# Attention steps of an MoE + attention + FFN kernel: ScalarE's copy of the turned weights moved ahead of the two exponentials of its step

## Chip, cores and metric

The kernel runs on one core of a Trainium2 chip. The metric is the device time of one execution in microseconds (us); lower is better. Five engines work side by side, each on its own in-order list of instructions, and they wait for each other by semaphores: TensorE (PE), VectorE (DVE), ScalarE (ACT), GpSimd (POOL), and SyncE (SP), which issues transfers.

## What is computed

The reference is a transformer block over 8 sequences of 512 tokens with 256 features: a mixture of experts with a ternary projection, then the attention that this change touches, then a quantised FFN. The attention has 16 heads of 64 features that share one key and one value (and a null key and value in front), a bias for each head, a causal mask and a padding mask:

```python
q = (xn @ Wq).reshape(b, n, H, DH).transpose(0, 2, 1, 3) * scale
kv = xn @ Wkv
k, v = (kv[..., :DH], kv[..., DH:])
...
sim = jnp.einsum('bhid,bjd->bhij', q, k)
...
sim = sim + bias
...
attn = jax.nn.softmax(sim, axis=-1)
out = jnp.einsum('bhij,bjd->bhid', attn, v)
out = out.transpose(0, 2, 1, 3).reshape(b, n, INNER)
out = out @ Wo
return layernorm(out, g_out)
```

## The kernel before

The program runs in stages: experts (to about 480 us of the profiled span), attention (`attention_phase`, about 480 to 1320 us), the two halves of the FFN (the rest). Matrices are fp32.

The attention phase works through 8 batches (one sequence each) of 32 steps. Four steps (`i % 4` = 0, 1, 2, 3) make one pair of heads; a step handles one block of 128 queries for both heads (`hh` = 0 and 1). By the causal mask a block needs 128, 512, 256 or 384 keys, in that order of the four steps (`ORDER = (0, 3, 1, 2)`). Batch 0 and batch 7 are written out by themselves, the six between them run in a hardware loop of two batches a turn. Every engine has the steps written out in the same order, and the stages of one block are spread over steps:

- step i: PE computes the scores of both heads (L1180, L1181) into `psS` (`ps_y` in the profile), one half for each head. DVE adds the bias and takes the row's extreme (`biased_max`, L1031, result `att_top`). ACT takes the exponential in place with a sum (`exps`, L893). PE may compute the scores of step i + 1 for a head only when DVE has read that head's scores of step i.
- step 4k + 3 and 4k + 4: ACT's `null_exp` (L905) and DVE's `totals` (L1047 to L1051) end the softmax sums of the pair.
- step i + 5 (`NLAG`): POOL multiplies the block by the inverse sum (`normalise`, L837).
- step i + 6 (`TLAG`): PE turns the block (`turn`, L1192, transposes of 128x128) into `psT` (`ps_up`), one half for each head. Head 0's half is copied to `pr` (`keep` in the profile) by ACT (`turned_out`, L901), head 1's half by DVE (its own `turned_out`, L1059).
- step i + 7 (`PLAG`): PE multiplies the turned weights with the values (`weighted`, L1202).

So in step i PE turns block J = i - 6 and ACT copies it. `psT` has no second buffer: PE's `turn` waits, for each half, until the copy of the block before has left it:

```python
for hh, ready in ((0, sem.pa_ready), (1, sem.pb_ready)):
    pe.wait_ge(sem.p_normed, 2 * J + hh + 1)
    if not known(J, 1):
        pe.wait_ge(ready, J)
```

`pa_ready` is counted up by ACT's copy, `pb_ready` by DVE's. Within a step PE runs scores, turn, weighted, and then, by the step, output projection (`project`, L1268), the next queries (`queries`), or one of the small products for the next batch. ACT's copy waits for `t_done` (the turn of head 0's half in the same step). Around the copy ACT has the first half of the queries (`query_hi`, L916, at the start of steps 4k + 2), the output copy (`outputs_t`, L911, at the start of steps 4k + 3), and, at the end of single steps, copies for the next batch or the one before (`null_weights` L948 in step 4, `normed_hi` L921 in 8 and 12, `keys_values` L927 in 16, ...). DVE has layer-norm pieces (L624 to L644) in steps 0 to 6 and 13 to 20.

Of the kernel before, what the change touches and what calls it, by code (L numbers as in the profile page):

```python
# [43 lines left out]
def known(v, least):  # L44

    return isinstance(v, int) and v < least
# [703 lines left out]
def attention_phase(nc, dram, w, ps, sem):  # L750
# [12 lines left out]
    TLAG, PLAG, NLAG = 6, 7, 5  # L763
    ORDER = (0, 3, 1, 2)
    with ExitStack() as ctx:
# [25 lines left out]
        def scores_of(pp, hh, q):  # L791
            return sc[:, pp, hh, CAUSAL[q]:CAUSAL[q + 1]]
# [8 lines left out]
        def lagged(b, i, lag):  # L801

            behind = i < lag
            return behind, STEPS * b + i - lag, (i - lag) % STEPS

        with nc.Block() as block:
# [80 lines left out]
            def _(act):  # L887
                def exps(I, i):
                    pp, q = i // 4 % 2, ORDER[i % 4]
                    for hh in range(2):  # L890
                        act.wait_ge(sem.ttr_done, 2 * I + hh + 1)
                        s = scores_of(pp, hh, q)
                        nc.scalar.activation(s, s, ACT.Exp, scale=-1.0, bias=top[:, pp, q, hh:hh + 1],  # L893
                                             accum_out=lsum[:, pp, q, hh:hh + 1]).then_inc(sem.exp_done, 1)

                def turned_out(J, j):
                    n = P * (ORDER[j % 4] + 1)
                    act.wait_ge(sem.t_done, 2 * J + 1)
                    if not known(J, 2):
                        act.wait_ge(sem.pv_done, J - 1)  # L900
                    nc.scalar.activation(pr[:, j % 2, 0, 0:n], psT[:, 0, 0:n], ACT.Copy).then_inc(sem.pa_ready, 1)  # L901
# [11 lines left out]
                def query_hi(n, pp):  # L913
                    act.wait_ge(sem.q_done, n + 1)
                    for hh in range(2):
                        nc.scalar.activation(q_hl[0:D, pp, hh], psB[hh * D:(hh + 1) * D], ACT.Copy  # L916
                                             ).then_inc(sem.qh_ready, 1)
# [42 lines left out]
                def step(b, i, par, behind, ahead):  # L960
                    n = PAIRS * b + i // 4
                    if i % 4 == 3 and (behind or i >= 11):
                        outputs_t(n - 2, i // 4 % 2)
                    if i % 4 == 2 and (ahead or i < STEPS - 4):
                        query_hi(n + 1, (i // 4 + 1) % 2)
                    exps(STEPS * b + i, i)
                    if i % 4 == 3:
                        null_exp(n, i // 4 % 2)
                    late, J, j = lagged(b, i, TLAG)
                    if behind or not late:  # L970
                        turned_out(J, j)
                    if behind and i == PNT + 1:
                        null_weights(b - 1)
                    if behind and i == OUT:
                        projected(b - 1)
                    if ahead:
                        for c in range(HC):
                            if i == XN[c] + 1:
                                normed_hi(b + 1, 1 - par, c)
                        if i == KV + 1:  # L980
                            keys_values(b + 1, 1 - par)
                        if i == VT + 1:
                            values(b + 1, 1 - par)
                        if i == NULL + 1:
                            null_scores(b + 1)
                        if i == NT + 1:
                            null_by_token(b + 1, 1 - par)
# [17 lines left out]
                for i in range(PLAG + 1):  # L1005
                    if i % 4 == 3:
                        outputs_t(PAIRS * B + i // 4 - 2, i // 4 % 2)
                    if i < TLAG:
                        _, J, j = lagged(B, i, TLAG)
# [1084 lines left out]
```

## Time and profile before

| | |
|---|---|
| median of 3 runs | 1495.69 us (1494.85 to 1497.03) |
| profiled execution | 1493.01 us, of it span 1491.1 us from first to last instruction |
| granted TensorE clock, mean | 0.950 |
| busy share of the span: PE, weight loads, DVE, ACT, POOL | 87%, 67%, 70%, 51%, 37% |

The profile lists for each engine its busy time, and how long it sat idle before a group of instructions and which instruction of which engine ended that idle time (the releaser). A timeline row gives the start in the span, the duration, the instruction, how many alike follow each other (x4), and in brackets the idle time before it. Matmuls are pipelined: with several in flight, a row covers them together.

### The profile page before, as it was taken

To read this page: it belongs to the slowest core of one execution; us is meant where nothing else is said; L and a number is where in the kernel's file an instruction comes from. 1 tells how busy PE (TensorE), PEld (TensorE's weight loads), DVE (VectorE), ACT (ScalarE), POOL (GpSimd) and SP (SyncE) were. 2 spreads that over 40 slices of the span, in tenths; PEclk is the share of its full clock that TensorE was granted. 3 is DMA by queue.
4 is the path that set the end of the run, shared out by engine and by line. 5 is a ranking of instruction groups with operands and counts; after the bars stand their busy time and mean duration, and the time that the engine had idled before them with its cause. 6 is when DMAs were issued, how large, how long until landed. Compare 5 with 4: busy or idle time off the path is not lost. (4 is left out here: it accounts for less than half of the span.)

```text
span 1491.1 us, 30048 instructions
## 1 busy us (share of the span) xinstructions
PE 1291.4 (87%) x8710; PEld 998.4 (67%) x8710; DVE 1040.3 (70%) x2788; ACT 760.9 (51%) x1940; POOL 554.7 (37%) x834
## 2 busy tenths in 40 slices
PE   4989989998945799999998999999999999953866
PEld 2877877787832577777776777777777788741223
DVE  5566666666554777777777778767877767762986
ACT  3222322232212566666666666666667666634853
POOL 1333232333232675444443344443443444510004
PEclk9999999999976899999999999999999999976987
DMA  6232211221125100000000000010000000202215
GB/s 224 79 107 100 85 60 54 99 85 40 46 76 184 58 1 2 1 23 9 2 29 4 2 30 2 2 31 2 1 30 2 15 2 2 73 1 66 65 48 178
DMA packets 51043, 71.55 MB, mean 48 GB/s; under 512 B 4497, under 2 KB 43665, under 8 KB 48850
## 3 DMA queue, kind: packets, MB, share of 16 engines
q1 hardware_dynamic: 50338, 69.60, 14.1%
q8 instruction: 69, 1.13, 0.3%
q14 instruction: 76, 0.62, 0.1%
q10 hardware_dynamic: 560, 0.20, 0.1%
HBM read 57.07 MB, written 12.72 MB: 47 GB/s over the span
## 5 line engine op out<-in xcount | busy, mean ns | idle before, releaser
L893 ACT ACTIVATE scores<-scores,att_top 128x128 f32<-128x128 f32 (+3 forms) x512 | 282.7, 553 | 268.6 <-DVE att_top L1031 268.5
L837 POOL TENSOR_SCALAR scores<-scores,att_rinv 128x128 f32<-128x128 f32 (+3 forms) x512 | 265.8, 536 | 203.8 <-DVE att_rinv L1049 203.8
L1031 DVE CUSTOM_DVE_ANT_0 scores<-ps_y,w_bias_b,null_s 128x128 f32<-128x128 f32 x448 | 229.6, 547 | 113.6 <-PE ps_y L1181 102.2
L261 POOL TENSOR_TENSOR act_w<-act_g,wide_w 128x512 f32<-128x512 f32 x64 | 105.6, 1650 | 282.5 <-DVE act_g L379 277.0
L1192 PE MATMUL ps_up<-ident,scores 128*128 128x128 f32 x1280 | 187.3, 275 | 26.5 <-ACT keep L901 26.1
L1202 PE MATMUL ps_a<-keep,w_val 128*64 128x128 f32 x2560 | 197.2, 284 | 0.3 <-DVE keep L1059 0.3
L1180 PE MATMUL ps_y<-k_hh,q_hl 128*128 128x256 f32 (+2 forms) x512 | 186.3, 374 | 12.7 <-DVE att_top L1031 5.9
L1192 PEld LDWEIGHTS ps_up<-ident,scores 128*128 128x128 f32 x1280 | 150.3, 140 | 49.9 <-issue 33.9
L208 ACT ACTIVATE hid_hi<-hid 128x512 fp32r<-128x512 f32 x80 | 50.5, 631 | 241.9 <-DVE hid L397 241.9
L844 POOL TENSOR_SCALAR w_q_hm<-q_hl 64x512 fp32r<-64x512 f32 x128 | 76.8, 612 | 256.2 <-ACT q_hl L916 256.2
L1202 PEld LDWEIGHTS ps_a<-keep,w_val 128*64 128x64 f32 x2560 | 135.2, 136 | 42.0 <-issue 38.1
L1181 PE MATMUL ps_y<-w_k_lm,w_q_hm 128*128 128x256 f32 (+2 forms) x512 | 162.1, 326 | 0.0
L1268 PE MATMUL ps_gate<-w_wo,o_t 128*128 128x256 f32 x512 | 145.9, 404 | 0.0
L1059 DVE COPY keep<-ps_up 128x128 f32<-128x128 f32 (+3 forms) x256 | 125.1, 489 | 12.8 <-PE ps_up L1192 7.2
L1180 PEld LDWEIGHTS ps_y<-k_hh,q_hl 128*128 128x128 f32 x512 | 97.2, 190 | 38.9 <-issue 22.2
L34 PE MATMUL ps_y<-w_down_hi,hid_hi 128*128 128x256 f32 x320 | 92.6, 289 | 26.9 <-DVE y L360 20.8
L901 ACT ACTIVATE keep<-ps_up 128x128 f32<-128x128 f32 (+3 forms) x256 | 108.0, 422 | 7.3 <-PE ps_up L1192 5.6
L379 DVE TENSOR_TENSOR act_g<-ps_gate,leak 128x512 f32<-128x512 f32 x80 | 55.3, 692 | 80.5 <-ACT leak L202 80.5
L1268 PEld LDWEIGHTS ps_gate<-w_wo,o_t 128*128 128x128 f32 x512 | 85.8, 189 | 27.6 <-issue 21.3
L1181 PEld LDWEIGHTS ps_y<-w_k_lm,w_q_hm 128*128 128x128 f32 x512 | 97.6, 191 | 7.9
L1069 DVE TENSOR_TENSOR q_hl<-ps_a,q_hl 64x512 fp32r<-64x512 f32 x128 | 88.2, 689 | 12.2 <-ACT q_hl L916 8.2
L893 ACT ACTIVATION_READ_ACCUMULATOR scores<-scores,att_top 128x1 f32 x512 | 95.8, 187 | 0.0
(236 smaller groups left out, 2596.1 us busy)
## 6 DMA issues: line engine op xcount, KB each, us to landing
wide_w<-token_w_dram SPq DMA_DIRECT2D x16, 1024.0 KB, 4.7
x_raw<-in_x_t_dram SPq DMA_DIRECT2D x8, 512.0 KB, 3.8
x_nat<-in_x_nat_dram SPq DMA_DIRECT2D x8, 512.0 KB, 4.8
x_dram<-x_nat SPq DMA_DIRECT2D x8, 512.0 KB, 2.9
w_x1t<-x_dram SPq DMA_DIRECT2D x8, 512.0 KB, 4.0
c_dram<-out_raw SPq DMA_DIRECT2D x8, 512.0 KB, 3.2
c2t<-c_dram SPq DMA_DIRECT2D x8, 512.0 KB, 3.7
x_tile<-x_dram SPq DMA_DIRECT2D x8, 512.0 KB, 4.4
```

The source lines that it names most:

```text
L34: pe.matmul(out, w_hi, x_hi, start=start, stop=False, skip_group_check=loose)
L261: nc.gpsimd.tensor_tensor(act_w[:, k % 2], act_g[:, k % 2], wide_w[:, k], ALU.mult).then_inc(sem.act_w_ready, 1)
L837: nc.gpsimd.tensor_scalar(s, s, rinv[:, pp, q, hh:hh + 1], 0.0, ALU.mult, ALU.add).then_inc(sem.p_normed, 1)
L893: nc.scalar.activation(s, s, ACT.Exp, scale=-1.0, bias=top[:, pp, q, hh:hh + 1], accum_out=lsum[:, pp, q, hh:hh + 1]).then_inc(sem.exp_don ...
L901: nc.scalar.activation(pr[:, j % 2, 0, 0:n], psT[:, 0, 0:n], ACT.Copy).then_inc(sem.pa_ready, 1)
L1031: dve.tensor_tensor_reduce(scores_of(pp, hh, q), psS[:, hh, 0:n], bias_of(w, h)[:, CAUSAL[q]:CAUSAL[q] + n], 1.0, null_s[:, par, q, h:h + ...
L1059: nc.vector.tensor_copy(pr[:, j % 2, 1, 0:n], psT[:, 1, 0:n]).then_inc(sem.pb_ready, 1)
L1180: pe.matmul(psS[:, hh, 0:n], q_hl[:, pp, hh, cols], k_hh[:, par, 0:n], start=True, stop=False)
L1181: pe.matmul(psS[:, hh, 0:n], q_hm[:, pp, hh, cols], k_lm[:, par, 0:n], start=False, stop=True).then_inc(sem.qk_done, 1)
L1192: last = pe.transpose(psT[:, hh, k * P:(k + 1) * P], s[:, k * P:(k + 1) * P], w.ident[:])
L1202: last = pe.matmul(psO[hh * D:(hh + 1) * D, cols], val[:, par, k], pr[:, j % 2, hh, k * P:(k + 1) * P], start=(k == 0), stop=(k == q))
L1268: last = pe.matmul(out, o_t[:, p % 2, cols], w.wo[:, p], start=(p == 0 and i == 0), stop=False, skip_group_check=True)
```

## The change

In ACT's `step`, `turned_out` is called before `exps` and not after it. Nothing else differs; all other engines have the same instructions in the same order.

```diff
                         query_hi(n + 1, (i // 4 + 1) % 2)
+                    late, J, j = lagged(b, i, TLAG)
+                    if behind or not late:
+                        turned_out(J, j)
                     exps(STEPS * b + i, i)
                     if i % 4 == 3:
                         null_exp(n, i // 4 % 2)
-                    late, J, j = lagged(b, i, TLAG)
-                    if behind or not late:
-                        turned_out(J, j)
```

The first place is on ACT in the batches of the hardware loop, steps 4 to 7 of a batch. L893 are the exponentials, L901 the copy out of `ps_up`, L948 and L949 the null weights of the batch before, L916 `query_hi`, L911 `outputs_t`. Before:

```order
L893 ACTIVATE scores,att_sum<-scores,att_top 128x128
L898 ISA
L901 ACTIVATE keep<-ps_up 128x256
L948 ACTIVATE w_null_nt<-ps_a 16x512
L949 ACTIVATE w_null_nt<-ps_a 16x512
L891 ISA
L893 ACTIVATE scores,att_sum<-scores,att_top 128x512
L891 REGISTER_ALU
L893 ACTIVATE scores,att_sum<-scores,att_top 128x512
L898 ISA
L901 ACTIVATE keep<-ps_up 128x384
L914 REGISTER_ALU
```

Now:

```order
L901 ACTIVATE keep<-ps_up 128x256
L891 ISA
L893 ACTIVATE scores,att_sum<-scores,att_top 128x128
L891 REGISTER_ALU
L893 ACTIVATE scores,att_sum<-scores,att_top 128x128
L948 ACTIVATE w_null_nt<-ps_a 16x512
L949 ACTIVATE w_null_nt<-ps_a 16x512
L898 ISA
L901 ACTIVATE keep<-ps_up 128x384
L891 ISA
L893 ACTIVATE scores,att_sum<-scores,att_top 128x512
L891 REGISTER_ALU
```

The copies of 256 columns (step 4) and of 384 columns (step 5) stand ahead of their step's exponentials; the null weights follow straight on the exponentials.

The second place is PE, where nothing moved: the order and the waits of two steps (4k and the start of 4k + 1) are these before and now.

```order
L1180 MATMUL ps_y<-k_hh,q_hl 128x256 [waits ttr_done]
L1181 MATMUL ps_y<-w_k_lm,w_q_hm 128x256
L1192 MATMUL ps_up<-ident,scores 128x128 [waits pa_ready,p_normed]
L1192 MATMUL ps_up<-ident,scores 128x128
L1192 MATMUL ps_up<-ident,scores 128x128 [waits pb_ready,p_normed]
L1192 MATMUL ps_up<-ident,scores 128x128
L1202 MATMUL ps_a<-keep,w_val 64x128 [waits pb_ready,pa_ready]
L1202 MATMUL ps_a<-keep,w_val 64x128 x7
L1180 MATMUL ps_y<-k_hh,q_hl 128x512 [waits ttr_done]
```

What moved is thus only when `pa_ready` is given, on which the first transpose of a turn waits.

## Rows read from the trace of the kernel before

**Rows 1.** Who waited for whom, whole run: us in total, times, longest

```profile
DVE scores L1031 <- PE ps_y L1181: 116.9, 105, 3.5
...
PE ps_up L1192 <- ACT keep L901: 26.1, 38, 1.5
```

**Rows 2.** Batch 3: length; PE, PEld, DVE, ACT, POOL busy; granted clock; DMA

```profile
793.70:897.20 103.50, 99.53 (x756) 78.99 (x757) 80.19 (x261) 67.97 (x204) 45.29 (x82) 1.00 0.04 12
```

**Rows 3.** Who waited for whom, batch 3 alone

```profile
PE ps_up L1192 <- ACT keep L901: 3.1, 4, 1.0
```

**Rows 4.** Timeline of batch 3, step 6: PE and ACT

```profile
813.39 0.39 PE L1180 MATMUL ps_y<-k_hh,q_hl 128*128 128x256 f32 x1 [0.16 <-DVE att_top L1031]
813.61 0.28 PE L1181 MATMUL ps_y<-w_k_lm,w_q_hm 128*128 128x256 f32 x1
...
814.12 0.47 ACT L901 ACTIVATE keep<-ps_up 128x384 f32<-128x384 f32 x1
...
814.74 0.52 PE L1192 MATMUL ps_up<-ident,scores 128*128 128x128 f32 x2 [0.84 <-ACT keep L901]
...
815.18 0.66 PE L1202 MATMUL ps_a<-keep,w_val 128*64 128x128 f32 x8
```

**Rows 5.** Timeline of batch 3, step 10: PE

```profile
826.73 0.28 PE L1181 MATMUL ps_y<-w_k_lm,w_q_hm 128*128 128x256 f32 x1
826.85 0.38 PE L1192 MATMUL ps_up<-ident,scores 128*128 128x128 f32 x2
827.15 0.33 PE L1202 MATMUL ps_a<-keep,w_val 128*64 128x128 f32 x2
```

**Rows 6.** Timeline of batch 3, steps 3 and 4: DVE and PE

```profile
806.14 0.69 DVE L1059 COPY keep<-ps_up 128x512 f32<-128x512 f32 x1
...
807.37 0.63 PE L1192 MATMUL ps_up<-ident,scores 128*128 128x128 f32 x4 [0.68 <-ACT keep L901]
```

**Rows 7.** Timeline of batch 3, steps 6 and 7: DVE and PE

```profile
816.91 0.29 DVE L1059 COPY keep<-ps_up 128x128 f32<-128x128 f32 x1
...
817.66 1.03 PE L1192 MATMUL ps_up<-ident,scores 128*128 128x128 f32 x8
```

**Rows 8.** Timeline of batch 3, steps 14 and 18 to 20: PE and DVE

```profile
840.05 0.52 PE L1192 MATMUL ps_up<-ident,scores 128*128 128x128 f32 x2 [0.55 <-ACT keep L901]
...
855.05 0.52 PE L1192 MATMUL ps_up<-ident,scores 128*128 128x128 f32 x2 [0.98 <-ACT keep L901]
...
860.23 0.69 DVE L1059 COPY keep<-ps_up 128x512 f32<-128x512 f32 x1
...
861.46 0.67 PE L1192 MATMUL ps_up<-ident,scores 128*128 128x128 f32 x4
```

**Rows 9.** Timeline after the last batch, where ACT waits for the turn

```profile
1311.09 1.04 PE L1192 MATMUL ps_up<-ident,scores 128*128 128x128 f32 x8
1311.73 0.60 ACT L901 ACTIVATE keep<-ps_up 128x512 f32<-128x512 f32 x1 [0.89 <-PE ps_up L1192]
```

**Rows 10.** Timeline of batch 3, steps 27 and 28: PE, ACT, DVE

```profile
883.07 1.03 PE L1192 MATMUL ps_up<-ident,scores 128*128 128x128 f32 x8
...
883.72 0.61 ACT L893 ACTIVATE scores<-scores,att_top 128x384 f32<-128x384 f32 x1 [0.72 <-DVE att_top L1031]
...
884.93 0.19 ACT L905 ACTIVATE null_p<-null_d 128x8 f32<-128x8 f32 x1
...
886.78 0.35 DVE L1031 CUSTOM_DVE_ANT_0 scores<-ps_y,w_bias_b,null_s 128x128 f32<-128x128 f32 x1
```

**Rows 11.** DVE in batch 3: its wait for the null weights, and a layer-norm piece twice

```profile
DVE w_null_nt L1063 <- ACT w_null_nt L949: 0.9, 1, 0.9
...
803.31 0.43 DVE L636 TENSOR_TENSOR w_work<-w_seed 128x4 f32<-128x4 f32 x1
...
806.92 0.16 DVE L636 TENSOR_TENSOR w_work<-w_work 128x4 f32<-128x4 f32 x1
```

**Rows 12.** Timeline of POOL around the first of those two pieces

```profile
802.68 2.07 POOL L837 TENSOR_SCALAR scores<-scores,att_rinv 128x256 f32<-128x256 f32 x4
```

## Prediction, made before the changed kernel ran

> **What bounds the kernel now.** I read the list of waits for the whole run first, then the busy times of one batch of the attention, then the timeline of that batch step by step. In the attention PE is the engine that the others follow: DVE's bias-and-extreme step waited 116.9 us in 105 places for PE's scores [rows 1], and in batch 3 PE was busy 99.53 of 103.50 us against 80.19 for DVE and 67.97 for ACT, at a granted clock of 1.00 [rows 2]. So time is gained where PE's few holes close, and only there. The largest group of holes is the one that the change aims at: before the transposes of a turn PE sat idle 26.1 us, in 38 places, until ACT's copy of the block before was out [rows 1]; in batch 3 this was 3.1 us in 4 places [rows 3].
>
> The timeline of step 6 shows how such a hole is made. PE issues its last score matmul at 813.61 and could go on to turn the next block. It starts at 814.74, because ACT's copy of step 5 only began at 814.12, behind that step's two exponentials of 512 columns, and ended at 814.59 [rows 4]. From the copy's end to the transpose is 0.15 us. An unhindered step of the same shape is step 10: last score 826.73, turn 826.85, weighted product 827.15, thus 0.42 us from score to product [rows 5]. In step 6 it is 815.18 - 813.61 = 1.57 us [rows 4]. The hole costs 1.57 - 0.42 = 1.15 us where the list says 0.84, since the pipeline has to fill again: idle time and 0.31 more. With that, all 38 holes are worth 26.1 + 38 x 0.31 = 37.9 us. This is the most that the change can return.
>
> **What the change does, part by part.**
>
> *No instruction is added or removed, and none moves on PE, DVE, POOL or SP.* ACT's copy of step i - 1 now runs before the exponentials of step i - 1. It needs only the turn of head 0's half. How soon that is shows behind the last batch, where ACT has nothing else to do: turn of 512 columns at 1311.09, copy at 1311.73, so 0.64 us later [rows 9]. The copy then ends some 1.2 us after the turn's start and is done before PE reaches the next step's turn everywhere (the steps are 2.1 us or longer: 103.50 / 32 = 3.2 on average, [rows 2]). So I take ACT's share of each hole as gone, 0 left. What takes its place is the question, because PE's turn has two halves and the second waits for DVE's copy, and PE's scores wait for DVE's extremes. Neither moves by itself. I walk through batch 3.
>
> *Steps 0 to 8.* DVE carries layer-norm pieces here and is itself close to the limit. In step 4 the hole is 0.68 us, with the turn at 807.37 [rows 6]. Transposes follow each other every 0.11 us (8 in 1.03 us less one of 0.27, over 7), so head 1's half began at 807.59. DVE's copy that it needs ran from 806.14 to 806.83 [rows 6]; with the 0.14 us of handover it could begin at 806.97. So after step 4 PE is ahead by at most 0.62 us, though the holes of steps 2 and 4 are worth more. In step 6 even that is lost: PE waits for DVE's extreme in the middle of the scores, at 813.39 [rows 4], and DVE was late by its own work. DVE gets a little earlier: its wait of 0.9 us for ACT's null weights in step 4 [rows 11] shortens by about 0.27, the distance by which the copy of 256 columns stands between exponential and null weights. Then the hole of step 6 (1.15) goes: ahead by 1.42. In step 7 head 1's half began at 817.66 + 0.44 = 818.10, and DVE's copy ended at 817.20 [rows 7], 816.93 with DVE's own 0.27; with the handover 817.07. So at most 1.03 us stays ahead. Step 8 repeats this in small; I take **0.9 us** for this part of the batch, where the holes of steps 4 and 6 alone are worth 0.99 + 1.15 = 2.14.
>
> *Step 14.* The hole is 0.55 [rows 8], with the refill 0.86 us. DVE is not late in the step after it by the timeline. **0.86 us.**
>
> *Steps 18 to 20.* The hole is 0.98 [rows 8], 1.29 with the refill. But two steps later head 1's half began at 861.46 + 0.25 = 861.71, and the DVE copy of step 19 ended at 860.92 [rows 8], so that 861.06 is the earliest: **0.65 us** stays. From step 21 on DVE has time to spare and follows.
>
> Sum for a batch: 0.9 + 0.86 + 0.65 = 2.4 us, where the listed idle time is 3.1 [rows 3]. The six batches of the hardware loop are alike: 6 x 2.4 = 14.4. The holes of batches 0 and 7 and the end are what is left of the 26.1, about 26.1 - 6 x 3.25 = 6.6 us; at the same share of return (2.4 / 3.1 = 0.77) 5.1, and I take 4.6, since DVE is late more often in batch 0. Sum: **19.0 us**.
>
> *What is put off.* The exponentials now stand behind the copy, and the copy behind PE's turn. In step 27 the turn starts at 883.07 [rows 10]; the copy could start at 883.71, and the exponentials 0.50 us later (0.60 of the copy [rows 9] less the 0.1 by which neighbours on ACT overlap), at 884.21 and not 883.72. The null exponential then ends at 885.12 + 0.49 = 885.61. Who waits for it is DVE's totals, behind its second extreme of step 28, at 886.78 + 0.28 = 887.06 [rows 10]. That leaves 1.4 us, so this costs nothing. Without that cover, DVE's in-order list would stop, and behind the totals stand the copy of head 1 and the next extreme, for which PE waits. Where ACT's exponentials were late because of DVE (steps 3 to 6, 13, 17) the copy falls into ACT's idle time and delays nothing. The copies at the end of steps 8, 12 and 16, which DVE waits for, follow after copy and exponentials in either order, so they start at the same time within 0.1 us.
>
> *A lock between DVE and POOL.* A layer-norm piece of four elements took 0.43 us at 803.31, and 0.16 us at 806.92 [rows 11]; during the first POOL was normalising, 802.68 to 804.75 [rows 12]. The Trainium skill (SBUF — State Buffer, "SBUF: two separate sides") says that a DVE instruction with two SBUF inputs and a GpSimd instruction exclude each other for the whole instruction. By that rule the change can lengthen DVE's chain, as POOL's query copies start when `query_hi` is through, which is now earlier; the trace agrees that such pieces stretch. By the row the stretch is 0.27 us a piece, and whether more or fewer pieces meet POOL cannot be read; I take 0 and make it a rival.
>
> The sum is made against the profiled execution of 1493.0 us, which gives 1474.0. The median of the runs shown is 2.7 us above that execution: 1495.69 - 19.0 = **1476.7 us**.
>
> **Rivals.**
>
> 1. *DVE's holds give way too.* If DVE's copies and extremes start earlier as PE does, more comes back than I allow: between 26 and 38 us, middle 30, time 1465.7. For it: DVE waits for PE 116.9 us in all. Against it: in steps 0 to 7 the timeline shows DVE at work without a break but one.
> 2. *The lock lengthens DVE's chain.* Three pieces of 0.27 us in each of the two DVE-bound parts of a batch are 0.8 us each; 2 x 0.8 x 8 = 13 us of the 19 would be gone: time 1489.7.
> 3. *DVE takes over the whole wait.* If head 1's copy and the extremes hold PE wherever ACT did, the holes only change their name: 1495.7. Against it: in step 14 no such hold is in sight.
> 4. *Slower: the exponentials come too late for the totals.* In each group of four steps the null exponential has 1.4 us to spare. If a turn (which also waits for POOL's normalised block) came more than 1.4 us later than I reckon, each of 64 groups would lose the excess. To eat the 19 us and lose 3 more, it takes 22 / 64 = 0.35 us beyond, so about 1.8 us late in every group: time 1499. Against it: no wait of a turn for POOL is in the list.
> 5. *The change does nothing.* The rows of the order show the swap in every step, so I give this no chance of its own.
>
> **How the numbers follow.** Chances: forecast 0.66 (its own range 14 to 25 us less, 1471 to 1482, as the holds of DVE may be half or one and a half of what I take); rival 1 0.12; rival 2 0.08; rival 3 0.08; rival 4 0.06. A difference of 0.2% (3 us) is about what a measurement of this kernel can tell. Faster: 0.66 + 0.12 + 0.08 = 0.86; same 0.08; slower 0.06. The range from 1465 to 1488 holds the forecast and most of rivals 1 and 2's side, and leaves out rivals 3 and 4.
>
> **What the profile of the changed kernel would show.** The wait of L1192 for ACT's copy is gone from the list, or below 3 us. In its place a wait of L1192 for DVE's copy (L1059) appears, some 5 to 15 us in all, in steps 4, 7 and 20, and the wait of L1180 for `att_top` grows in step 6. ACT's own idle time moves from before L893 to before L901 (released by PE). A batch takes about 101.1 us. PE's busy time stays. I am wrong if batches take as long as before with as much idle time before L1192 (rival 3), if the pieces of layer norm get longer (rival 2), or if DVE's totals (L1047) show a wait for `null_p` (rival 4).

## The result, and the profile after

The changed kernel took **1473.94 us** (median of 4 runs, 1473.23 to 1475.61) beside 1496.36 us (4 runs, 1494.85 to 1499.34) for the kernel before on the same chip: a ratio of 0.9846, 95% interval 0.9828 to 0.9864. The prediction was 1476.7 us, with a range of 1465 to 1488 and a chance of 0.86 for faster. The profiled execution took 1475.61 us against 1493.01, so 17.4 us less. By the traces the attention (from the first score matmul of batch 0 to the last weighted product in step 31 of batch 7) is the whole of it.

The windows of the attention, before and after: length, then PE, PEld, DVE, ACT and POOL busy with instruction counts, granted clock, DMA share, GB/s.

```profile
480.60:1304.30 823.70, 780.34 (x5870) 619.25 (x5872) 629.02 (x2022) 536.80 (x1605) 385.81 (x714) 0.99 0.05 16
```

```profile
481.00:1286.10 805.10, 780.21 (x5872) 616.77 (x5872) 628.35 (x2022) 543.84 (x1606) 384.21 (x714) 0.99 0.05 17
...
787.10:887.90 100.80, 99.32 (x756) 78.58 (x756) 79.91 (x261) 69.25 (x202) 45.08 (x82) 1.00 0.04 12
```

The attention is 18.6 us shorter, at the same PE work (780.34 and 780.21 us) and the same clock: only idle time went. The rest of the span is 667.4 us before and 668.5 after; in it the steps behind batch 7, which turn and multiply the last blocks, end 0.4 us earlier too, so that up to the very last weighted product the gain is 19.0 us (837.0 to 818.0). The last row is batch 3, 100.80 us where it was 103.50 [rows 2].

The list of waits of the kernel after, whole run (us in total, times, longest):

```profile
ACT keep L901 <- PE ps_up L1192: 153.2, 158, 3.2
DVE scores L1031 <- PE ps_y L1181: 103.9, 98, 3.3
ACT scores L893 <- DVE att_top L1031: 88.9, 80, 3.4
...
PE ps_up L1192 <- DVE keep L1059: 6.2, 22, 1.1
PE ps_y L1180 <- DVE att_top L1031: 5.9, 10, 3.1
...
DVE att_sum L1047 <- ACT null_p L905: 0.6, 1, 0.6
```

No row of L1192 waiting for ACT's copy is left; it was 26.1 us in 38 places [rows 1]. What PE lost to DVE in its stead is 6.2 us in 22 places. Of these, 2.8 us lie in batch 0 alone. ACT now waits for PE's turn in front of its copy (153.2 us), where nothing is behind it in a hurry. DVE's totals wait for the null exponential (L1047) once, 0.6 us, behind batch 7, and PE waits once for POOL's block before a turn (L1192, 0.4 us, batch 7, step 19); before, neither wait was in the list.

The timeline of batch 3 after, at the places that the prediction walked through (start, us, engine, line, operation; in brackets the idle time before and who ended it):

```profile
796.71 0.16 DVE L636 TENSOR_TENSOR w_work<-w_seed 128x4 f32<-128x4 f32 x1
...
799.27 0.69 DVE L1059 COPY keep<-ps_up 128x512 f32<-128x512 f32 x1
...
799.57 0.38 PE L1192 MATMUL ps_up<-ident,scores 128*128 128x128 f32 x2
800.11 0.41 PE L1192 MATMUL ps_up<-ident,scores 128*128 128x128 f32 x2 [0.17 <-DVE keep L1059]
...
803.22 0.68 DVE L1063 TENSOR_TENSOR w_null_nt<-ps_a,w_null_nt 16x512 fp32r<-16x512 f32 x1 [0.61 <-ACT w_null_nt L949]
...
806.26 0.39 PE L1180 MATMUL ps_y<-k_hh,q_hl 128*128 128x256 f32 x1 [0.17 <-DVE att_top L1031]
...
806.61 0.52 PE L1192 MATMUL ps_up<-ident,scores 128*128 128x128 f32 x2
...
809.79 0.29 DVE L1059 COPY keep<-ps_up 128x128 f32<-128x128 f32 x1
...
848.92 0.63 PE L1192 MATMUL ps_up<-ident,scores 128*128 128x128 f32 x4 [0.17 <-DVE keep L1059]
...
852.45 0.41 PE L1192 MATMUL ps_up<-ident,scores 128*128 128x128 f32 x2 [0.18 <-DVE keep L1059]
...
873.79 1.03 PE L1192 MATMUL ps_up<-ident,scores 128*128 128x128 f32 x8
...
874.43 0.60 ACT L901 ACTIVATE keep<-ps_up 128x512 f32<-128x512 f32 x1 [0.72 <-PE ps_up L1192]
874.92 0.61 ACT L893 ACTIVATE scores<-scores,att_top 128x384 f32<-128x384 f32 x1
...
876.12 0.19 ACT L905 ACTIVATE null_p<-null_d 128x8 f32<-128x8 f32 x1
...
877.78 0.17 DVE L1047 TENSOR_TENSOR att_sum<-att_sum,null_p 128x8 f32<-128x8 f32 x1
```

In step 4 the turn starts at once (799.57), but its second half waits for DVE's copy, which ends at 799.96. In step 6 the turn has no idle time before it (0.84 us before [rows 4]); the hold by the extreme in the middle of the scores is as it was. Steps 19 and 20 have the small holds by DVE's copy. In step 27 the copy stands in front of the exponentials, and DVE still has 1.47 us between the end of the null exponential (876.31) and its totals (877.78).

### The profile page after: what moved, and what is told of

The parts are those of the page before. It is cut to its first block and busy times, and to the rows that moved or that the text cites. A ratio compares the mean times of both kernels' runs of the same rounds, so it can differ in the third digit from the quotient of the medians.

```text
span 1473.6 us, 30046 instructions
## 1 busy us (share of the span) xinstructions
PE 1290.3 (88%) x8705; PEld 996.1 (68%) x8710; DVE 1039.8 (71%) x2788; ACT 767.6 (52%) x1940; POOL 553.1 (38%) x834
## 5 line engine op out<-in xcount | busy, mean ns | idle before, releaser
L893 ACT ACTIVATE scores<-scores,att_top 128x128 f32<-128x128 f32 (+3 forms) x512 | 281.5, 553 | 89.2 <-DVE att_top L1031 88.9
L1031 DVE CUSTOM_DVE_ANT_0 scores<-ps_y,w_bias_b,null_s 128x128 f32<-128x128 f32 x448 | 229.4, 547 | 100.5 <-PE ps_y L1181 89.1
L1192 PE MATMUL ps_up<-ident,scores 128*128 128x128 f32 x1280 | 191.7, 274 | 8.2 <-DVE keep L1059 6.2
L1180 PE MATMUL ps_y<-k_hh,q_hl 128*128 128x256 f32 (+2 forms) x512 | 187.6, 376 | 12.8 <-DVE att_top L1031 5.9
L901 ACT ACTIVATE keep<-ps_up 128x128 f32<-128x128 f32 (+3 forms) x256 | 111.9, 437 | 156.1 <-PE ps_up L1192 153.2
L1192 PEld LDWEIGHTS ps_up<-ident,scores 128*128 128x128 f32 x1280 | 150.3, 140 | 30.9 <-issue 10.4
L1181 PE MATMUL ps_y<-w_k_lm,w_q_hm 128*128 128x256 f32 (+2 forms) x512 | 162.7, 327 | 0.0
L1059 DVE COPY keep<-ps_up 128x128 f32<-128x128 f32 (+3 forms) x256 | 125.1, 489 | 11.2 <-PE ps_up L1192 5.5
L1180 PEld LDWEIGHTS ps_y<-k_hh,q_hl 128*128 128x128 f32 x512 | 97.4, 190 | 41.0 <-issue 21.3
L1181 PEld LDWEIGHTS ps_y<-w_k_lm,w_q_hm 128*128 128x128 f32 x512 | 97.7, 191 | 8.0
L893 ACT ACTIVATION_READ_ACCUMULATOR scores<-scores,att_top 128x1 f32 x512 | 96.8, 189 | 0.0
```

What stands on the lines that cost most here:

```text
L1031: dve.tensor_tensor_reduce(scores_of(pp, hh, q), psS[:, hh, 0:n], bias_of(w, h)[:, CAUSAL[q]:CAUSAL[q] + n], 1.0, null_s[:, par, q, h:h + ...
L1059: nc.vector.tensor_copy(pr[:, j % 2, 1, 0:n], psT[:, 1, 0:n]).then_inc(sem.pb_ready, 1)
L1180: pe.matmul(psS[:, hh, 0:n], q_hl[:, pp, hh, cols], k_hh[:, par, 0:n], start=True, stop=False)
L1181: pe.matmul(psS[:, hh, 0:n], q_hm[:, pp, hh, cols], k_lm[:, par, 0:n], start=False, stop=True).then_inc(sem.qk_done, 1)
L1192: last = pe.transpose(psT[:, hh, k * P:(k + 1) * P], s[:, k * P:(k + 1) * P], w.ident[:])
```

## The experiments

Each was timed beside the kernel before on the same chip, and the ratio is to that. Differences between experiments of a few us are read from the traces too, where the attention's parts show to 0.01 us what the medians blur. A whole trace is a single execution, though: stretches of half TensorE clock (last section) and the start of the attention, which lies between 478.7 and 484.0 us, differ from trace to trace, so where they matter, parts without them are compared.

### 1. The change once more

No edit.

> The change as it is, timed again beside the kernel before. My walk through the steps gave 19.0 us less; the traces of the two kernels show 18.6 us less in the attention and 1.1 us more around it, while the medians differ by 22.4. If the attention is all, this gives 17 to 20 us less. Rival: the change also returns something outside the attention that the single traces miss; then 22 us or more less.

Measured: 1473.35 us (5 runs, 1473.02 to 1475.86) beside 1497.16 (16 runs, 1493.04 to 1500.8): ratio 0.9844, interval 0.9827 to 0.9862. The median gain is 23.8 us, on the rival's side of the bound; in the trace the attention is 806.0 us, 17.7 less than before's, on the theory's. The two don't agree on the size, and the last section comes back to it. That the change gains 17 us or more is certain.

### 2. DVE's copy directly behind its extremes

```diff
                     biased_max(b, i, par)
+                    late, J, j = lagged(b, i, TLAG)
+                    if behind or not late:
+                        turned_out(J, j)
                     if i % 4 == 3:
                         null_shift(n, i // 4, par)
...
-                    late, J, j = lagged(b, i, TLAG)
-                    if behind or not late:
-                        turned_out(J, j)
```

> The change, and VectorE's copy of head 1's half moved directly behind the two extremes of its step, ahead of the null shift, the totals and the second half of the queries. PE now waits 6.2 us for that copy. Theory: this wait only shows that VectorE's whole chain is late in steps 3 to 8 and 18 to 20; in steps 7 and 19 the copy comes 1.4 us earlier, but PE is then held one step later by the copies of steps 7 and 19, which come only some 0.2 us earlier, or by the extremes. So 0 to 3 us less than the change, the wait for att_top grows. Rival: the wait is the place of one instruction, all 6.2 us come back: 6 us less than the change or more.

Measured: 1470.23 us (5 runs, 1465.22 to 1473.72), ratio 0.9818, interval 0.9795 to 0.9841; 3.1 us less than the change beside it. The list of waits of this kernel has no row of L1192 waiting for DVE, and one that grew:

```profile
PE ps_y L1180 <- DVE att_top L1031: 7.7, 16, 3.2
```

So 6.2 us of holds went, and 1.8 came back as waits for the extremes (5.9 with the change). The attention is 799.1 us, 6.0 less than with the change. The span is only 3.6 shorter, as the attention begins 3.0 us later in this trace. Batches 3 and 5 are as long as with the change (100.83 and 101.04 against 100.83 and 100.82); the gain lies in the even batches (2: 102.91 against 104.16; 4: 102.45 against 103.90; 6: 100.69 against 101.61), in batch 0 (99.21 against 101.06) and in batch 7 (0.7 us). In batches 3 and 5 the hold was DVE's chain and not the place of its copy: it only moved to the next extreme. There the theory holds. For the whole it was too low: the median, 3.1 us less, is just beyond its 0 to 3, and the attention's 6.0 us are at the rival's bound. In batch 0 the holds of steps 11 and 12, 0.4 and 1.1 us, were the place of the one copy and are gone.

### 3 and 4. Half of the change: only the copies of 384 columns ahead, only those of 512

```diff
-                    if behind or not late:
+                    if i % 4 == 1 and (behind or not late):
                         turned_out(J, j)
                     exps(STEPS * b + i, i)
                     if i % 4 == 3:
                         null_exp(n, i // 4 % 2)
+                    if i % 4 != 1 and (behind or not late):
+                        turned_out(J, j)
```

The second has `== 3` and `!= 3`.

> Only the copies of the steps 4k+1 (384 columns) are moved ahead of the exponentials; the others stay behind them. These copies close the holes of steps 2, 6, 14 and 18, by the refill-corrected list about 3.8 of 4.8 us of a batch. Theory of holds: in step 8 PE is then held by ACT's copy of step 7 (in the trace of before it ended at 820.77, where the hole-free turn would start about 0.9 earlier), in step 20 by that of step 19, both still behind exponentials that VectorE's chain makes late; so the gains of steps 6 and 18 are lost again and only step 14's 0.86 us stays: about 0.9 x 7 and some in batches 0 and 7, 7 to 9 us less than before, 1487 to 1489. Rival, holes simply add: 0.8 of the whole, 15 to 18 us less, 1478 to 1481.

> Only the copies of the steps 4k+3 (512 columns) are moved ahead. They close the holes of steps 4, 8 and 20. Theory of holds: what step 4 gives (0.6 us) is lost in step 6, where PE waits for VectorE's extreme and then for ACT's copy of step 5, so 0 to 0.2 us of a batch, and 1 to 3 us in batches 0 and 7: 1 to 4 us less than before. With the other half alone this makes 8 to 13 us, well under the 19 to 22 of both together. Rival, holes add: 4 to 5 us less, and the two halves make up the whole.

Measured: 1489.20 us (6 runs, 1486.66 to 1491.89), ratio 0.9948 (0.9931 to 0.9966), and 1491.17 us (11 runs, 1488.05 to 1499.67), ratio 0.9968 (0.9953 to 0.9983). These are 8.0 and 6.0 us less than before, 14.0 together, where the whole change gave 23.8 by the same medians. From the list of waits, of the first (in both kernels L1192 of the others is L1194, and DVE's L1059 is L1061):

```profile
PE ps_up L1194 <- ACT keep L901: 19.5, 26, 1.5
```

and of the second:

```profile
PE ps_up L1194 <- ACT keep L901: 18.6, 27, 1.0
...
PE ps_up L1194 <- DVE keep L1061: 2.0, 5, 1.1
```

Each half takes only a quarter of the idle time away (6.6 and 7.5 us of 26.1), because PE, once ahead by the hole that was closed, runs into the next step's copy that was left behind the exponentials. In batch 3 of the first, step 14's hole is gone and stays gone (steps 9 to 16 take 23.33 us for 24.18), but what step 18 gave is lost in steps 19 and 20, where PE again starts 0.14 us behind the end of ACT's copy (steps 16 to 22: 20.30 us for 20.28). By the medians the first lies 0.2 us beyond the theory's range, and the second gained 6.0 us, more than the theory (1 to 4) and the rival (4 to 5) had. The traces say less: the attention takes 820.5 and 823.9 us, 3.2 less and 0.2 more than before. Each of these two traces has two stretches of half clock at the start of batches 3 and 5; with steps 0 and 1 of these two batches left out on both sides, the gains are 6.3 and 2.9 us, where the whole change gives 18.6. So the second fits the theory by its trace, and why its median is 3 us better isn't known. By either measure the two halves together give no more than six tenths of the whole: the holes aren't additive; closing one class only passes the wait on.

### 5. The copy between the two exponentials

```diff
                 def exps(I, i, block=None):
...
                         if hh and block:
                             turned_out(*block)
```

> ScalarE's copy stands between the two exponentials of its step, not ahead of both. Theory of holds: it is enough that the copy ends before PE would start the next turn without a hole. In step 5 it would end about 1.3 us into step 6, 0.3 us after the turn wants to start, elsewhere in time; what that costs is mostly hidden behind VectorE's holds. So 0 to 2 us more than the change, 1473.5 to 1475.5, and a wait of L1192 for ScalarE's copy of 1 to 4 us. Rival: the gain needs the copy in ScalarE's idle time ahead of both exponentials; then about half is lost, 1483 to 1487.

Measured: 1479.88 us (6 runs, 1477.17 to 1480.91) beside 1495.79 (11 runs), ratio 0.9893, interval 0.9873 to 0.9912. It lies between theory and rival: 6 us slower than the change (7 by the ratios). In the trace the attention is 810.5 us, 5.4 more than with the change, of which a stretch of half clock at the start of batch 3 accounts for some 1.5. Its list of waits shows both engines:

```profile
PE ps_up L1192 <- ACT keep L903: 3.9, 14, 0.3
...
PE ps_up L1192 <- DVE keep L1059: 2.9, 5, 1.2
```

One exponential in front of the copy is enough to be late by up to 0.3 us in 14 places, in steps 4 and 18 of most batches. The 3.9 us of waiting are what the theory had (1 to 4), but they cost more than it allowed. I had taken the holes as larger than one exponential and so as closed either way; where PE has been let ahead in the steps before, they aren't. In batch 5, steps 0 to 9 take 0.5 us more than with the change and 9 to 16 0.24 more. The order matters by halves, in the sense in which the change has it.

### 6 and 7. Without DVE's layer-norm pieces in the attention: before, and after

```diff
-                    last = layer_norm(nc.vector, x1t, stat, mean_var, work, seed, stages)
...
-                        last.then_inc(sem.ln_ready, 1)
+                        nc.vector.nop(nofuse=True).then_inc(sem.ln_ready, 1)
```

The same in `norm_out`. Both kernels leave out the layer norm of the next batch's input and of the finished batch's output, that of the last batch too, which stands behind the attention; the expectation of the first says "except the last batch", and that is wrong of the kernel as it ran.

> The kernel before, with the layer-norm pieces of both kinds left out of VectorE's steps (statistics, inverse root and scaling are not computed for the attention's input from batch 1 on, nor for its output except the last batch). Theory: these pieces make the extremes, hence the exponentials, hence the copy late in steps 1 to 7; the holes of steps 2, 4 and 6 go, those of steps 14 and 18 stay, as there the extremes are late because of the key and feature copies. About 2.4 us for each of 7 or 8 batches: 1476 to 1481.

> The changed kernel with the same layer-norm pieces left out. Theory: the holes of steps 14 (0.86) and 18 (1.29) are closed by the change, and without layer norm VectorE no longer holds PE in steps 19 and 20, so 2.1 us for each of 7 batches: 13 to 16 us less than the kernel before without layer norm. Rival: all holes come from layer norm; then the change gives 0 to 4 us here.

Measured: 1466.19 us (4 runs, 1463.8 to 1467.67), ratio 0.9803, and 1444.50 us (4 runs, 1444.08 to 1447.47), ratio 0.9665. The first fell below its bounds by 10 us: some 6 of these are the last batch's layer norm (the span outside the attention is that much shorter), the other 4 are in the attention (802.0 us, 21.7 less than before's), where batch 0 alone gave 5.0 us and I had 2.4 for each batch. The swap alone is then worth 21.7 us by the medians and 20.9 by the attention (802.0 to 781.1), where 13 to 16 were expected and 18.6 are measured with DVE's pieces in. The list of waits of the first and of the second (in both, L1190 and L1178 are L1192 and L1180 of the other kernels):

```profile
PE ps_up L1190 <- ACT keep L901: 16.8, 26, 1.5
```

```profile
PE ps_up L1190 <- DVE keep L1059: 2.7, 4, 1.8
PE ps_y L1178 <- DVE att_top L1031: 2.6, 4, 1.6
...
PE ps_up L1190 <- ACT keep L901: 0.4, 1, 0.4
```

I expected fewer holes by ACT, as its exponentials would come earlier, and there are fewer (16.8 us in 26 places): in the batches of the loop those of steps 2 and 4 are gone, that of step 6 is 0.30 us for 0.84, where I had it gone too, and those of steps 14 and 18 stay. With DVE's pieces out of the way most of their worth comes back when they are closed. By the prediction's own rule they are worth 16.8 + 26 x 0.31 = 24.9 us, and 20.9 came back, 0.84 of it; with DVE's pieces in it was 18.6 of 37.9, 0.49. Batch 5 shows it best. Without the pieces it has three such holes of 1.83 us in sum, and closing them gives 2.76 us (101.06 to 98.30), just 1.83 + 3 x 0.31. With the pieces it has four, 3.05 us and by the rule worth 4.29, and closing them gives 2.64. In its steps 16 to 22 the swap gives 1.24 us without the pieces (20.12 to 18.88) and 0.65 with them. So in the batches of the loop DVE's layer-norm pieces are what withholds the rest, 1.65 of 4.29 us in batch 5; in batches 0 and 7 other holds remain, and no run separates them.

### 8 and 9. The output pieces moved out of the steps where they hold PE

Both on top of experiment 2. The first, and the second against it:

```diff
-        OUT, SCALE_OUT, LARGEST = 12, (21, 22), (23, 24)
+        OUT, SCALE_OUT, LARGEST = 12, (27, 28), (29, 30)
-        NORM_OUT = (13, 14, 15, 16, 17, 18, 19, 20)
+        NORM_OUT = (13, 14, 15, 22, 23, 24, 25, 26)
```

```diff
-        OUT, SCALE_OUT, LARGEST = 12, (27, 28), (29, 30)
+        OUT, SCALE_OUT, LARGEST = 12, (25, 26), (27, 28)
-        NORM_OUT = (13, 14, 15, 22, 23, 24, 25, 26)
+        NORM_OUT = (13, 14, 15, 21, 22, 22, 23, 24)
```

> The change, VectorE's copy behind its extremes as in the second experiment, and the last five of the eight layer-norm pieces of the output moved from steps 16 to 20 to steps 22 to 26, with what follows them (scaling 27 and 28, largest value 29 and 30). Theory: in steps 18 to 20 VectorE's chain holds PE back by 0.65 us of the 1.29; with the pieces gone from there this comes back, 0.5 to 0.7 us for each of 7 batches, and steps 22 to 26 have time for them: 3 to 5 us less than the second experiment, 1465 to 1467. Rival: the key copies alone set VectorE's chain in steps 17 to 20; then no change, 1470.

Measured: 1473.89 us (4 runs, 1472.97 to 1474.58), ratio 0.9857, interval 0.9836 to 0.9879: a miss, 4 us slower than without the move (6 by the ratios). In the trace the attention is 802.6 us, 3.5 more. Steps 16 to 22 of batch 3 did what was said (18.89 us for 19.6), yet steps 0 to 9 grew: to 29.27 us in batch 3 and 29.88 in batch 5, from 27.8 and 28.0, and to 29.0 to 29.4 in batches 2, 4 and 6, from 27.9. The row of the list of waits for DVE's idle time that nothing but issue ended:

```profile
DVE scores L1031 <- issue: 12.0, 11, 4.9
```

and the timeline of the same kernel at the start of batch 2, and at the turn of the hardware loop in front of batch 3, SyncE, DVE, ACT and PE:

```profile
684.71 1.41 DVE L624 BATCH_NORM_STATS2 w_stat<-w_x1t 128x6 f32<-128x256 f32 x4 [1.12 <-DMA w_x1t<-x_dram]
...
781.78 1.33 SPq L812 DMA_DIRECT2D w_x1t<-x_dram  x1
...
782.58 0.17 DVE L1039 TENSOR_TENSOR null_d<-att_top,null_s 128x8 f32<-128x8 f32 x1
786.54 0.35 DVE L1031 CUSTOM_DVE_ANT_0 scores<-ps_y,bias_a,null_s 128x128 f32<-128x128 f32 x1 [3.79 <-issue]
786.72 0.38 ACT L901 ACTIVATE keep<-ps_up 128x256 f32<-128x256 f32 x1 [3.72 <-PE ps_a L1202]
...
784.28 0.28 PE L1181 MATMUL ps_y<-w_k_lm,w_q_hm 128*128 128x256 f32 x1
...
786.95 0.50 PE L1180 MATMUL ps_y<-k_hh,q_hl 128*128 128x512 f32 x1 [0.69 <-DVE att_top L1031]
```

In front of batch 3 PE has the first scores at 784.56, and DVE takes them at 786.54: it finished its last step late and was then without work for 3.79 us (4.91 before batch 5), which nothing else releases. PE then waits for the extreme. In the other traces DVE's idle time at this place is 2.77 to 3.53 us and PE ends it by the list. In three of these places (experiments 2, 9 and 10) DVE takes the scores 0.4 us later than else, after 3.13 to 3.24 us, so there its own turn seems to take that long, and not 3.79 or 4.91. The next run tests whether a DVE that is done in time mends this. ACT, too, stands still here, for 3.72 us (4.65 with issue as its cause before batch 5).

Two more things went wrong in this kernel, and the theory of the next run leaves them out. SyncE loads the next batch's input only behind the store of the output, and the store waits for the largest values, now in steps 29 and 30. So the load reaches over the batch's end: in batches 2, 4 and 6, with no turn of the loop in front, DVE's first layer-norm piece waits 1.12, 1.45 and 1.07 us for it, and in no other trace does it wait for the load. Whether store and load also lengthen the turn of the loop, at which they are under way only in this kernel, no run tells. And in batch 5 the first step runs at half clock and takes 3.71 us with no wait of PE in it, as it does at half clock in experiments 3, 5 and 6 (3.61 to 3.67) without a late DVE.

> This is the previous kernel (DVE's copy directly behind the extremes, output layer-norm pieces moved out of steps 16 to 20) with the same pieces two steps earlier: its pieces in steps 13, 14, 15, 21, 22 (two), 23 and 24, the scaling in steps 25 and 26, the largest values in steps 27 and 28 (there 22 to 26, 27 and 28, 29 and 30). Theory: the previous kernel lost its gain at the turn of the loop, because DVE finished step 31 late and its own turn of the loop (3.8 and 4.9 us without work before batches 3 and 5, released by nothing but issue) then stood in front of the first extremes instead of beside PE's turn. With DVE done in time, the turn is hidden again, steps 0 to 9 of batches 3 and 5 go back from 29.3 and 29.9 us to about 27.9, steps 16 to 22 keep their 18.9 us (19.6 in the change), and the kernel takes 1465 to 1468 us, 3 to 5 us less than with DVE's copy first alone (1470.2). Rival: it is the moved pieces themselves that cost DVE's chain as much as they gave, wherever they stand, and the time is 1471 us or more. The half-clock stretches that some executions show (about 1.3 us each) can blur this by one or two us, so the attention's own length in the trace decides: 795 to 797 us by the theory (799.1 with DVE's copy first, 802.6 in the previous kernel).

Measured: **1465.59 us** (5 runs, 1464.23 to 1467.93) beside 1495.49 (11 runs), ratio 0.9802, interval 0.9782 to 0.9821. The attention is 795.8 us, inside the 795 to 797 expected; steps 0 to 9 are back at 27.80 and 28.04 us in batches 3 and 5 and at 27.9 in batches 2, 4 and 6, and steps 16 to 22 keep 18.87. At the same turn in this kernel:

```profile
781.83 0.17 DVE L1039 TENSOR_TENSOR null_d<-att_top,null_s 128x8 f32<-128x8 f32 x1
785.29 0.35 DVE L1031 CUSTOM_DVE_ANT_0 scores<-ps_y,bias_a,null_s 128x128 f32<-128x128 f32 x1 [3.30 <-PE ps_y L1181]
```

DVE now waits for PE, not PE for DVE, and its waits for issue before L1031 are 3.3 us in 9 places in the whole run. Its idle time there is no longer than in the kernels with the pieces in their old place. So the pieces cost little where they now stand; they cost more than they gave when they ended too late for the batch's end. The rival is refuted. That the turn of the loop was the whole loss, as the theory had it, is not shown: the load of the input is back in time as well (it lands at 679.68, before batch 2 begins at 681.85), and this trace has no stretch of half clock at the turns. This is the fastest of the kernels that leave nothing out, 8 us below the change's medians, or 7 by the ratios.

### 10. Experiment 2 once more, beside the last one

> The change with DVE's copy directly behind the extremes, measured a second time beside the kernel above on the same chip, since its 3.1 us over the change came from one set of runs. Theory: 1469 to 1472 us, attention 798 to 801 us, and the kernel above is 3 to 5 us faster than this one. Rival: the first value was a lucky set, and it takes 1473 us or more, as the change does.

Measured: 1467.24 us (6 runs, 1463.77 to 1473.63), ratio 0.9818, interval 0.9793 to 0.9843, the same ratio as the first time, so the rival (1473 us or more) is refuted. Time and attention (796.6 us) are both below what was expected, 1469 to 1472 and 798 to 801. By the medians experiment 9 is only 1.7 us faster than this, below the 3 to 5 expected, and the intervals of the two ratios overlap. In batches 1 to 6 it is 3.5 us shorter (605.6 against 609.1 us), as expected, and what blurs it is batch 0, 98.70 against 96.38 us, where the two kernels do the same. The last section has the causes.

### 11. The kernel before once more

No edit, for a second trace of before.

> The kernel before once more, for a second trace. Its runs spread from 1493.0 to 1500.8, those of the change from 1473.0 to 1475.9, and the trace shown was one of the fastest of before. Guess: the spread comes from stretches of half TensorE clock after the idle time at the loop's turn, as two experiments showed in the attention (1.4 us each); then this trace has one or two such stretches if its time is above 1495, and none if it is near 1493. Rival: the spread is spread over all stages.

Measured: 1497.21 us, attention 826.0 us against 823.7, with one stretch at half clock in batch 3, which took 104.81 us for 103.52. So the guess holds for 1.3 of the 4.2 us that its span is longer.

## Why the prediction was right, point by point

- *What bounds it.* PE in the attention: shown. PE's busy time didn't change, its idle time fell, and all of the profiled gain is there.
- *ACT's share of each hole is gone, 0 left.* Right: no such wait is in the list. Experiment 5 shows that less of an advance wouldn't have done.
- *Each hole is worth idle time and 0.31 us.* Held up in step 14, which nothing hinders after: steps 9 to 16 take 0.96 us less, forecast 0.86. In batch 5 of experiments 6 and 7 three holes of 1.83 us gave 2.76, which idle time alone could not.
- *Steps 0 to 8, 0.9 us.* Measured 1.05 in batch 3 (28.81 to 27.76), and 0.71 in each of batches 2, 4 and 6 (29.17 to 28.46 in batch 2), so the batches are not alike, and the mean of 0.88 is nearer to the forecast than any of them. DVE's copy of step 3 starts 12.18 us into the batch and not 12.44 [rows 6]. The prediction let this copy stand where it was, so its bound of 0.62 us behind step 4 was too low: PE is 0.87 ahead there. The 0.26 us are the layer-norm piece of step 2, which took 0.43 us beside POOL [rows 11] and takes 0.16 now. The shorter wait for the null weights comes later, in step 4: 0.61 us for 0.87, a gain of 0.26 (forecast 0.27). Both together make DVE's copy of step 7 0.51 us earlier in the batch (22.70 against 23.21 [rows 7]), where I allowed 0.27.
- *Steps 18 to 20, 0.65 us.* Measured 0.66 in batch 3 (20.28 to 19.62). That DVE holds here because of its layer-norm pieces is shown by experiments 7 and 9, where another 0.6 and 0.7 us come back.
- *Six batches, 14.4 us; batches 0, 7 and the end, 4.6.* Measured 14.75, and 3.86 in batches 0 and 7 with 0.4 behind them. The sum was 19.0 against 18.6 in the attention (19.0 with the end) and 17.4 for the profiled execution, as the rest of the span takes 1.1 us more (0.7 in the second trace of the change). That the terms meet the measured ones to some tenths is in part luck: an unforeseen gain and loss by the lock (below) partly cancel, and batches 0 and 7 were never walked through. The median fell by 22.4, 3.4 more than the sum. The sum speaks of the traces, and the trace of before lies 3.4 us below its median (1493.0 and 1496.4) while that of the change lies 1.7 above (1475.6 and 1473.9); for this difference the prediction has no term, and the last section comes back to it.
- *What is put off costs nothing.* Forecast 0.49 us of delay and 1.4 us to spare before DVE's totals; the exponential in step 27 starts 0.49 us behind the copy's start, and 1.47 us were to spare. Only behind batch 7 did the totals wait, 0.6 us once, the sign of rival 4. The copy starts 0.64 us behind the turn, as in [rows 9].
- *The lock between DVE and POOL, 0.* Right in sum, as DVE's busy time in the attention is 628.35 us for 629.02, but not in the single batch. The piece of four elements in step 2 (0.41 to 0.44 us before, in all six batches of the loop) takes 0.16 in batches 1, 3 and 5 and 0.51 to 0.52 in batches 2, 4 and 6. With it goes what step 4 gives, 0.51 and 0.52 us in the first three and 0.17 to 0.19 in the others. By that term, put at 0 for want of a row, the odd batches gained some 0.27 us each and the even ones lost some 0.08.
- *The signs.* The new wait for DVE's copy is 6.2 us (forecast 5 to 15), in batch 3 in steps 4 and 20 and, unforeseen, in step 19; without the 2.8 us of batch 0 the sum would be below the forecast; in step 7 it shows only as a longer turn (1.32 us for 1.03). The wait of L1180 for `att_top` did not grow in sum (5.9 us in 10 places): wrong, since PE and DVE both come to that place of step 6 0.52 us earlier in the batch (19.17 us in, against 19.69 [rows 4]). A batch of 101.1 us: 100.8.
- *The rivals.* None occurred. Rival 1 (DVE's holds give way by themselves) comes nearest; experiments 2 and 9 show that they give way only when DVE's program is changed, 7 to 8 us more (9.3 in the attention).

## What to carry to other kernels

A copy that frees a buffer for the bounding engine goes ahead of work that nobody waits for yet; price it by walking to the next hold of each other engine, since here only half of what the holes were worth came back, and DVE's pieces withheld most of the rest in the loop's batches. Move all of such copies, as half of them gives less than half. Work moved off to the end of a loop's body can cost more than where it stood: look at when that engine gets to the next batch, and at the transfers that wait for the work, when the batch's start gets longer.

## What the runs showed of the hardware

**A turn of a hardware loop** left PE without work for 1.42 to 2.36 us in all thirteen traces, with nothing but issue as its cause (the bracket of its first score matmul). DVE stood for 2.77 to 3.53 us, which PE ended by the list, and in experiment 8 for 3.79 and 4.91 us with issue as the cause. It is seen before batches 3 and 5, and not before 2, 4 and 6: a pass of the loop holds two batches. What makes it longer in experiment 8 stays open.

**Half clock after PE's turn of the loop.** In seven of the thirteen traces (the kernel before's second one, experiments 3, 4, 5, 6, 7, 8) one or two stretches at a granted clock of 0.5, thus 1.2 GHz, begin between 0.2 us before and 1.6 us after the end of PE's idle time at the loop's turn, and in the other six there is none. Experiment 3, PE's timeline (L1182 and L1183 are L1180 and L1181 of the other kernels):

```profile
791.85 0.38 PE L1182 MATMUL ps_y<-k_hh,q_hl 128*128 128x256 f32 x1 [2.10 <-issue]
...
795.13 0.63 PE L1183 MATMUL ps_y<-w_k_lm,w_q_hm 128*128 128x512 f32 x1
```

and its windows, with the granted clock as the third number from the end:

```profile
793.30:797.00 3.70, 3.70 (x22) 2.88 (x19) 3.18 (x13) 0.91 (x5) 2.06 (x4) 0.54 0.00 0
797.00:805.00 8.00, 8.00 (x61) 6.37 (x60) 6.41 (x22) 5.02 (x14) 3.25 (x6) 1.00 0.01 3
```

A matmul of 512 columns takes 0.63 us there and 0.40 elsewhere, and the batch is some 1.3 us longer (104.81 against 103.52 in the two traces of before). The idle time doesn't decide it: 2.36 us in front of batch 3 of before had no such stretch behind it. The Trainium skill (TensorE: Matmul & The Clock Gate, "Part 1: The HAM clock gate") says that the watch over PE's activity runs freely and isn't reset by a kernel, so that the same kernel meets it in another phase each time; that the stretches come and go between executions of one kernel (none in the first trace of before, one in its second) agrees with it. It is part of the spread between runs. Whether it is the reason why the medians differ by 22 to 24 us and the traces by 17 to 18 stays open: before's first trace, at 1493.0 us, is near the lower edge of its runs, both traces of the change, at 1475.6 and 1475.9 us, are the slowest of theirs, though they have no such stretch, and before's second, with one stretch, is at 1497.2, with 2.3 of the 4.2 us more in the attention and 1.9 outside it, which I can't place. Between before's second trace and the change's first the executions differ by 21.6 us.

**DVE and POOL exclude each other.** In batch 0 two layer-norm pieces of DVE took 2.99 us in experiment 9:

```profile
503.20 2.99 DVE L644 TENSOR_SCALAR w_x1t<-w_x1t,w_mean_var,w_work 128x256 f32<-128x256 f32 x2
...
504.79 1.25 POOL L601 TENSOR_SCALAR w_bias_b<-w_bias_b 128x1280 f32<-128x1280 f32 x1
```

and 1.79 in experiment 10:

```profile
503.57 1.79 DVE L644 TENSOR_SCALAR w_x1t<-w_x1t,w_mean_var,w_work 128x256 f32<-128x256 f32 x2
...
505.08 1.38 POOL L601 TENSOR_SCALAR w_bias_b<-w_bias_b 128x1280 f32<-128x1280 f32 x1
```

In the one DVE's second piece came behind POOL's instruction of 1280 columns, ending at 506.19 with POOL's at 506.04; in the other both were through at 505.36, while POOL's ran on to 506.46. PE waited 3.0 and 1.8 us for them, so 1.2 of the 2.3 us by which batch 0 differs. The Trainium skill (SBUF — State Buffer, "SBUF: two separate sides") has this as a lock that the one which starts first holds for its whole instruction, where DVE's is in a mode that takes both ports or has two SBUF inputs; the rows agree, though none shows in which mode these pieces ran. The prediction counted it in pieces of 0.27 us; in batch 0 one meeting costs 1.2. The rest of the 2.3 us is the clock. In experiment 9 step 8 follows on PE's wait of 2.96 us, runs at half clock and takes 3.72 us; in experiment 10 it follows on 1.76 us, at full clock, and takes 2.51. The windows of the two:

```profile
507.00:510.40 3.40, 3.40 (x22) 3.07 (x24) 2.67 (x12) 3.10 (x11) 0.69 (x3) 0.50 0.01 2
```

```profile
506.20:508.60 2.40, 2.40 (x24) 1.77 (x24) 2.18 (x10) 2.31 (x10) 1.39 (x5) 1.00 0.01 3
```
